# Rows of f2 scores by transposing a broadcast column, and routed rows of the first sixteen batches gathered inside the expert stage

## What is computed

```python
# experts: top 2 of softmax(x @ Wr), weights renormed; y = shared(x) + sum_e w_e * expert_e(x)
def _gat(inp, adj_mask, W, a):
    h = inp @ W;  f1 = h @ a[:F_, 0];  f2 = h @ a[F_:, 0]
    e = leaky_relu(f1[:, :, None] + f2[:, None, :], 0.2)      # masked in the second one
    return elu(softmax(e, axis=2) @ h)
out = relu(x @ mlp1_w + mlp1_b)                               # 256 wide
out = elu(_gat(relu(out), None, W_fc, a_fc)) + out
out = relu(out @ mlp2_w + mlp2_b)                             # 128 wide
out = elu(_gat(relu(out), adj, W_hand, a_hand)) + out;  return relu(out)
```

## Time and profile before

| what | us |
|---|---|
| median of 3 runs (1116.24 to 1118.69) | 1116.54 |
| the profiled execution | 1119.85 |
| its span, first to last instruction | 1118.1 |
| PE busy | 975.7 |
| DVE busy | 737.7 |
| ACT busy | 675.1 |
| POOL busy | 481.2 |

### The profile page before, as it was taken

The page is one execution under the profiler, slowest core; times in us unless marked ns, Lnnn a source line. Parts: engine busy times, 40 slices in busy tenths (PEclk is TensorE's granted clock), DMA queues, the critical chain, the costliest instruction groups (busy, mean ns, idle before and its releaser), DMA issues. The chain is left out here.

```text
span 1118.1 us, 25162 instructions
## 1 busy us (share of the span) xinstructions
PE 975.7 (87%) x7980; PEld 817.2 (73%) x7980; DVE 737.7 (66%) x2234; ACT 675.1 (60%) x1670; POOL 481.2 (43%) x474
## 2 busy tenths in 40 slices
PE   1698999997999999999999925899999998459998
PEld 1577888886667799999999922666666665349997
DVE  4678888885650145555545523588898896569998
ACT  4445666654433446666656613688888887467773
POOL 2545666651154654444400057677766722011111
PEclk9879999999999999999999966999999999779999
DMA  7900100112613137766565411111111100001011
GB/s 201 373 6 32 47 38 38 38 40 77 175 58 121 53 115 206 206 207 201 175 180 176 127 47 47 30 36 30 32 34 29 32 5 1 1 1 39 29 38 47
DMA packets 91705, 94.14 MB, mean 84 GB/s; under 512 B 16336, under 2 KB 69712, under 8 KB 90448
## 3 DMA queue, kind: packets, MB, share of 16 engines
q1 hardware_dynamic: 71936, 50.40, 14.4%
q10 hardware_dynamic: 11472, 25.63, 7.9%
q0 software_dynamic: 8192, 16.79, 4.9%
HBM read 52.54 MB, written 33.96 MB: 77 GB/s over the span
## 5 line engine op out<-in xcount | busy, mean ns | idle before, releaser
L1548 POOL DMA_INDIRECT g_y<-slot_rows_out,slots x128 | 129.6, 1012 | 141.3 <-SPq L1977 92.1
L1283 POOL DMA_INDIRECT slot_rows_in<-xn_all,slots x128 | 129.7, 1013 | 136.8 <-DMA slot_rows_in<-xn_all,slots 93.6
L1170 ACT ACTIVATE s_hT<-s_hp,expert 128x256 f32<-128x256 f32 x284 | 111.8, 476 | 54.6 <-PE s_hp L1161 54.5
L1183 PE MATMUL s_yp<-w_experts,s_hT 128*128 x1136 | 138.0, 275 | 0.0
L1183 PEld LDWEIGHTS s_yp<-w_experts,s_hT 128*128 128x128 f32 x1136 | 132.8, 192 | 0.0
L1191 DVE TENSOR_TENSOR xnT_all<-s_yp,expert 128x256 f32<-128x256 f32 x71 | 30.1, 424 | 117.7 <-PE s_yp L1183 117.7
L489 DVE SCALAR_TENSOR_TENSOR l_mi<-l_sbc,mT 128x512 bf16<-128x512 f32 x128 | 84.5, 670 | 7.1 <-PE l_sbc L480 5.9
L1159 PE MATMUL s_hp<-e_xh,e_wh 128*128 128x256 f32 x284 | 86.6, 305 | 0.0
L1082 ACT ACTIVATE s_hT<-s_hp,b_shared 128x512 f32<-128x512 f32 x64 | 44.0, 687 | 65.3 <-PE s_hp L1065 63.7
L1160 PE MATMUL s_hp<-e_xl,e_wh 128*128 128x256 f32 x284 | 80.5, 284 | 0.0
L1161 PE MATMUL s_hp<-e_xh,e_wl 128*128 128x256 f32 x284 | 80.5, 284 | 0.0
(11 more groups left out here) (323 smaller groups left out, 2652.7 us busy)
## 6 DMA issues: line engine op xcount, KB each, us to landing
expert<-expert_rows ACTq DMA_DIRECT2D x65, 322.0 KB, 3.1
slot_rows_in<-zeros SPq DMA_DIRECT2D x9, 1024.0 KB, 12.8
xnT_all<-slot_rows_in SPq DMA_DIRECT2D x71, 128.0 KB, 3.1
slot_rows_out<-xnT_all SPq DMA_DIRECT2D x71, 128.0 KB, 2.3
xn_all<-l_xr SPq DMA_DIRECT2D x16, 256.0 KB, 2.3
xnT_all<-l_rT SPq DMA_DIRECT2D x16, 256.0 KB
out_dram<-f_ot SPq DMA_DIRECT2D x16, 256.0 KB, 2.3
w_experts<-in_L_ffn_W2p_dram SPq DMA_DIRECT2D x8, 256.0 KB, 3.8
```

What stands on the lines that cost most here:

```text
L1170: nc.scalar.activation(hT[q % 2][:, c, :], hp[:, c, 0:TILE], ACT.Gelu, bias=wt[q][:, F + c:F + c + 1]).then_inc(s["h_ok"], 1)
L1183: ins = pe.matmul(yp[q % 2][:, h * D:(h + 1) * D], hT[q % 2][:, c, h * P:(h + 1) * P], w2, start=(c == 0 and h == 0), stop=(c == FC - 1), ...
L1283: pool.indirect_dma_start(k.rows_in, bass.IndirectOffsetOnAxis(ap=k.slots[:, c, b:b + 1], axis=0), k.xn[:, b, :], None).then_inc(scattered ...
L1548: pool.indirect_dma_start(y_slot[c][:, b, :], None, k.rows_out, bass.IndirectOffsetOnAxis(ap=k.slots[:, c, b:b + 1], axis=0))\
```

## The change

Four parts.

1. Both f2 rows are made from the h products: a second extra column is f2 as a column, and a PE transpose of this column, broadcast over 128 columns, gives it as a row on all partitions. Four transposes of 128 columns take the place of the products of 512 columns (two with a 256-deep weight for b, one for d). They read h1 and h2 in SBUF, and so wait for their evictions. w_f2_fc and w_f2_hand go, with the two copies that filled them.
2. PE's order: the f2 of d moves behind b_sums, the f2 of b behind the transposes of p2 and the dense layer of a.
3. Rows of batches 0 to 15 are gathered in the expert stage, by POOL, behind the scatter, once the last tile that holds such rows is stored (a place worked out from the slot counts by DVE, PE and DVE; y_ok is the gate). All gathered rows now lie in xn_all and xnT_all. The graph stage gathers groups 4 to 15 only, group 4 at its start, group g + 6 in step g.
4. slot_rows_out is zeroed in the attention stage by nine 1 MB DMAs on SP's queue, one behind the saves of each of the first nine groups.

```diff
                 for g in range(GROUPS):
                     sp_keep(sp, g)
+                    if g < k.zero_dmas:
+                        some = rows[:, 2048 * g:min(2048 * g + 2048, rows.shape[1])]
+                        sp.dma_start(some, k.zeros[:, 0:some.shape[1]]).then_inc(k.out_zeroed, 16)
...
+GATHERED_EARLY = 2
+def slot_rows(k, c, b):
+    return k.xn[:, b, :] if c == 0 else k.xnT[:, (b + 2 * AHEAD * TILE // P) % BATCHES, :]
...
         def pe_table(pe):
             pe.wait_ge(s["marks"], 1)
+            pe.transpose(counts[0:EC, 16:16 + J], last_of[:], k.ident[0:J, 0:J])
...
+                pool.wait_ge(s["table"], 1)
+                for n in range(TOPK * CHUNK * EC):
+                    b, c = n // TOPK, n % TOPK
+                    if n % (TOPK * CHUNK) == 0:
+                        at = b // CHUNK
+                        stored = pool.value_load(last_at[at:at + 1, 0:1], min_val=1 + U, max_val=TILES + U)
+                        pool.wait_ge(s["y_ok"], stored)
+                        pool.tensor_tensor(gather_fence[:, at:at + 1], k.ones[:, 0:1], k.ones[:, 0:1], ALU.mult)
+                    wait(pool, early[c], 16 * b)
+                    if n % IN_A_ROW == 0:
+                        wait(pool, early[1 - c], 16 * b)
+                    pool.indirect_dma_start(
+                        slot_rows(k, c, b), None, k.rows_out,
+                        bass.IndirectOffsetOnAxis(ap=k.slots[:, c, b:b + 1], axis=0)).then_inc(early[c], 16)
...
+                fold(dve.tensor_scalar(after_place[:], place[:], float(1 + U), None, ALU.add))
+                fold(dve.scalar_tensor_tensor(holds[:], counts[here, 128:128 + EC * EXPERTS]
+                                              .rearrange("p (c e) -> p c e", e=EXPERTS), j_start[here],
+                                              after_place[:].unsqueeze(1).to_broadcast([J, EC, EXPERTS]),
+                                              ALU.is_gt, ALU.mult))
+                dve.tensor_reduce(last_of[:], holds[:], AX.X, ALU.max)
...
+                fold(dve.tensor_reduce(last_f[:], counts[0:EC, 16:16 + J], AX.X, ALU.max))
+                dve.tensor_copy(last_at[:], last_f[:])
...
                 tiles(dve_slot, dve)
+                for q in range(U):
+                    dve.wait_ge(out[q], 16 * len(range(q, TILES, U)))
+                dve.memset(store_fence[:], 0.0).then_inc(s["y_ok"], U)
...
-W1C = FD + 1
+W1C = FD + 2
-W2C = D + 1
+W2C = D + 2
...
         def pe_b_f2(pe, g, p):
             wait(pe, s["y1_ok"], g)
             wait(pe, s["y2_ok"], g - 1)
-            for c in range(H1):
-                ins = pe.matmul(ff[:], k.w_f2_fc[:, c, :], r1T[p][:, c, :], start=(c == 0), stop=(c == H1 - 1))
+            for b in range(GB):
+                wait(pe, s["h1_ok"], g * GB + b + 1)
+                ins = pe.transpose(ff[:, b * P:(b + 1) * P], h1[p][:, b, FD + 1:FD + 2].to_broadcast([P, P]), k.ident[:])
             ins.then_inc(s["f1_ps"], 1)
...
-            pe.matmul(ff[:], k.w_f2_hand[:], r2T[p][:], start=True, stop=True).then_inc(s["f2_ps"], 1)
+            wait(pe, s["h2_ok"], g + 1)
+            for b in range(GB):
+                ins = pe.transpose(ff[:, b * P:(b + 1) * P], h2[:, b, D + 1:D + 2].to_broadcast([P, P]), k.ident[:])
+            ins.then_inc(s["f2_ps"], 1)
...
             if on["d"]:
                 pe_d_h2(pe, g, p)
-                pe_d_f2(pe, g, p)
             if on["c"]:
                 pe_b_sums(pe, g + 1, q)
+            if on["d"]:
+                pe_d_f2(pe, g, p)
             if on["b"]:
                 pe_b_h1(pe, g + 2, p)
             if on["a"]:
                 pe_a_transpose(pe, g + 3)
-            if on["b"]:
-                pe_b_f2(pe, g + 2, p)
             if on["d"]:
                 pe_d_transpose(pe, g)
             if on["a"]:
                 pe_a_dense(pe, g + 3)
+            if on["b"]:
+                pe_b_f2(pe, g + 2, p)
...
-                pool_gather(pool, 0, range(8))
-                for g in range(-4, GROUPS):
+                pool_gather(pool, FIRST, range(8))
+                for g in range(-2, GROUPS):
                     on = stages(g)
-                    more = g + 5 < GROUPS
+                    more = -1 <= g < GROUPS - FIRST - 2
                     if more:
-                        pool_gather(pool, g + 5, range(0, 6))
+                        pool_gather(pool, g + FIRST + 2, range(0, 6))
```

More of the change, by code:

```diff
@@ L812, in _ @@
                 sp.wait_ge(k.slots_zeroed, 16 * k.zero_dmas)
+                rows = k.rows_out.rearrange("(p n) d -> p (n d)", p=P)
                 for g in range(GROUPS):
                     sp_keep(sp, g)
+                    if g < k.zero_dmas:
+                        some = rows[:, 2048 * g:min(2048 * g + 2048, rows.shape[1])]
+                        sp.dma_start(some, k.zeros[:, 0:some.shape[1]]).then_inc(k.out_zeroed, 16)
+                sp.wait_ge(k.out_zeroed, 16 * k.zero_dmas)
                 sp.wait_ge(s["xr_kept"], 16 * GROUPS)
@@ L881, in persistent @@
     k.slots_zeroed = ctx.enter_context(nc.semaphore("slots_zeroed"))
+    k.out_zeroed = ctx.enter_context(nc.semaphore("out_zeroed"))
     k.zero_dmas = 9
@@ L993, in experts_phase @@
         pool_fence = sb("r_pool_fence", [P, CHUNKS])
+        EC = GATHERED_EARLY
+        j_start, after_place = sb("r_j_start", [P, 1]), sb("r_after_place", [J, EXPERTS])
+        holds, last_of = sb("r_holds", [J, EC, EXPERTS]), sb("r_last_of", [J, EC])
+        last_f, last_at = sb("r_last_f", [EC, 1]), sb("r_last_at", [EC, 1], I32)
+        store_fence, gather_fence = sb("r_store_fence", [P, 1]), sb("r_gather_fence", [P, EC])
         s_hT = [sb(f"s_hT{p}", [P, FC, GB * P]) for p in range(2)]
@@ L1020, in experts_phase @@
         scattered = [sem(f"m_scattered{p}") for p in range(2)]
+        early = [sem(f"m_early{c}") for c in range(TOPK)]
         x_in = [sem(f"m_x_in{q}") for q in range(U)]
@@ L1288, in _ @@
                 pool.memset(pool_fence[:, CHUNKS - 1:CHUNKS], 0.0).then_inc(s["arrived"], 1)
+                pool.wait_ge(s["table"], 1)
[12 more added lines that the diff above has]
+                        bass.IndirectOffsetOnAxis(ap=k.slots[:, c, b:b + 1], axis=0)).then_inc(early[c], 16)
+                for c in range(TOPK):
+                    pool.wait_ge(early[c], 16 * CHUNK * EC)
             @block.scalar
@@ L1493, in combine_graph_phase @@
         G4 = [P, GB, P]
-        y_slot = [sb(f"y{c}", [P, BATCHES, D]) for c in range(TOPK)]
+        FIRST = GATHERED_EARLY * CHUNK // GB
         st, fence, lnv = sb("st", [P, GB, 6]), sb("fence", [P, 1]), sb("lnv", [P, GB])
@@ L1540, in pool_gather @@
         def pool_gather(pool, g, which):
+            later = g - FIRST
             for n in which:
@@ L1544, in pool_gather @@
                 if n < TOPK:
-                    wait(pool, gathered[1 - g % 2][c], 16 * GB * ((g + 1) // 2))
+                    wait(pool, gathered[1 - g % 2][c], 16 * GB * ((later + 1) // 2))
                 else:
-                    wait(pool, gathered[g % 2][c], 16 * (GB * (g // 2) + n // TOPK))
-                pool.indirect_dma_start(y_slot[c][:, b, :], None, k.rows_out,
+                    wait(pool, gathered[g % 2][c], 16 * (GB * (later // 2) + n // TOPK))
+                pool.indirect_dma_start(slot_rows(k, c, b), None, k.rows_out,
                                         bass.IndirectOffsetOnAxis(ap=k.slots[:, c, b:b + 1], axis=0))\
@@ L1552, in dve_n_combine @@
         def dve_n_combine(dve, g, half, p, c):
-            wait(dve, gathered[p][c], (half + 1) * 16 * GB)
+            wait(dve, gathered[p][c], (half + 1 - FIRST // 2) * 16 * GB)
             if c == 1:
@@ L2006, in _ @@
                     if more:
-                        pool_gather(pool, g + 5, range(6, 8))
+                        pool_gather(pool, g + FIRST + 2, range(6, 8))
                     if on["b"]:
@@ L2283, in build @@
                 experts_phase(nc, k, a)
-        combine_graph_phase(nc, k)
+            combine_graph_phase(nc, k)
         last_ffn_phase(nc, k, out)
```

13 lines of the change are left out of this document (5 added, 8 removed).

## The result

The changed kernel takes 1190.96 us (median of 4 runs, 1190.74 to 1193.69), the kernel before 1116.39 beside it (4 runs, 1106.9 to 1118.69): 1.0691 times as long, 95% interval 1.0627 to 1.0754. Forecast were 1182 and a range of 1152 to 1206. The profiled execution took 1190.86 us, its span is 1189.1, 71.0 more than before. The page first: busy time by engine, then tenths in 40 slices of some 30 us.

A forecast was written before the change was run, and what follows sets the result against it. It took the ring of handovers through ACT, not PE throughput, as the bound. Loop 58.6, ramp -14.8 and clock 22 gave +65.8 us, 1185.7 for the profiled execution, 1182 as median; range 1152 to 1206.

The forecast's parts named there:

- The ring: Graph loop: handovers among ACT, DVE, POOL and PE bound the 16.77 us step; later operands for ACT lengthen it fully.
- d side: Graph loop: f2 of d behind b_sums lets ACT begin y2 1.2 us late each step.
- b side: Graph loop: f2 of b behind p2 transposes and dense layer lets ACT begin y1 3.1 us late each step.
- Step 13: Graph loop step without a dense layer on either side: 4.2 - 1.7 = 2.5 us longer.
- step 14: Graph loop step with only the d delay: 1.2 us longer.
- The ramp: Graph stage start to first h2: earlier gathers save 9.0 and 8.2 us, late f2 costs 1.2 twice: -14.8 us.
- The clock: Graph loop: new PE gaps lower the granted clock, a little over one fall a step, 1.6 x 14 = 22 us.
- Rival (b): Graph loop: the clock falls at both gaps in each step, 41 us for 22, total 1201; chance 0.15.
- Rival (a): Graph loop: the granted clock holds, +43.8 us, total 1160; chance 0.27.
- Costed at nothing: Early gathers behind the scatter, their gate's work and the nine zero DMAs: taken as 0 us.
- rival (d): Expert stage: early rows come too late as the gate opens with the last tile, +17.2, total 1199; chance 0.04.
- rival (e): Attention stage: zero DMAs delay the saves by some us each, +10 to 20, total 1197; chance 0.03.

The follow-up runs named there:

- e10: Changed kernel with unread products filling PE's three gaps and gathers of groups 5 to 15 left out: 1161.73 us, 1.038 times the kernel before.
- e8: Changed kernel with PE's old order, f2 of d as a product, f2 of b as transposes: 1096.28 us, 0.9815 times the kernel before.
- e11: Changed kernel with f2 of d back behind h2 and products filling the gaps before p2's and r2T's transposes: 1144.87 us, 1.0263 times the kernel before.
- e5: Changed kernel with two unread products of 512 columns in each of PE's three gaps: 1174.11 us, 1.0441 times the kernel before.
- e9: Changed kernel with fourteen transposes of ident in each of PE's three gaps: 1170.67 us, 1.0392 times the kernel before.
- e1: Changed kernel with both f2 rows as products in PE's old order, early gathers and zeroing kept: 1094.8 us, 0.9799 times the kernel before.
- e6: Changed kernel with f2 of b back between the transposes of xn and p2: 1136.73 us, 1.0115 times the kernel before.
- e3: Changed kernel with its f2 transposes kept but PE's order as before: 1104.02 us, 0.9886 times the kernel before.
- e7: Changed kernel with f2 of d back right behind h2, f2 of b still late: 1192.73 us, 1.0608 times the kernel before.

## Why the prediction was right, step by step

**The ring, and PE at 93% not the bound.** Shown: a step at full clock is 21.03 (forecast 16.77 + 4.2 = 21.0), e10 gives it with PE 93% busy, e8 gives 16.73 with PE 86% busy. The reading behind it, that ACT's small waits are the latency of a ring and no slack, held.

**d side 1.2, b side 3.1.** ACT's waits are 1.29 and 3.05 us, and by the step lengths (e11's table) it is 1.29 and 3.07. The prediction's 1.2 for the d side is kind and place in one: of the 1.29 the place behind b_sums is 0.93, and 0.36 is what the transposes cost over the product even right behind h2. The 0.46 us for four transposes of a broadcast column, which had no row, is 719.23 - 718.79 = 0.44. Step 13, forecast at 16.77 + 2.5 = 19.3, takes 18.6 in e5, e9 and e10; step 14, at 18.0, takes 17.9 (its clock is low in the kernel before too, 0.80, and 0.71 here). The fifteen without the new falls of the clock, 13 x 21.03 + 18.6 + 17.9, make 309.9 us, 58.3 over 251.57; of the 58.6 forecast 58.3 belong to these fifteen. e10 measures the same stretch with 311.7 us.

**The ramp.** -15.5 for -14.8, but as two misses that nearly cancel: without late f2 rows (e1) it is 43.1 - 62.44 = -19.3 where I had -17.2, and the f2 rows add 46.89 - 43.1 = 3.8 where I had 2.4.

**The clock: the term that was mis-sized.** 22 us were forecast, 343.63 - 309.9 = 33.7 came. The price of a fall, up to 1.45 us, was near (1.50 and 1.55, and 0.31 more behind them); their number was not. I took 1.6 us a step, a little over one fall; ten of the thirteen full steps are 2.7 us or more above 21.03, one is 0.75 above, and only two have none. Rival (b), a fall at both gaps of each step at 41 us, names the mechanism better than my count does, and the time lies about midway between its 1201 and my 1182. I had given weight against it to the stretch 952:957, where PE was idle and the clock stayed: one gap at the loop's end told little of gaps that return each step. Rival (a), the clock at 1.00 and 1160 us, did not happen; e10, at 1161.73, is about that kernel, its gathers aside. The gaps before the p2 and the r2T transposes are the ones with slow work behind them, as the prediction had it; the one before the third h1 product, 1.78 us, has none in any step of the changed kernel (it has in e6, where it grows to 3.5 us).

**Costed at nothing.** The gathers behind the scatter ended 23.6 us before POOL's next work, though each took 2.1 us for 1.4: rival (d) is out. The attention phase ended 1.37 us earlier than before (278.49 for 279.86, SP's mark), and SP waited 124.6 us for xr where it waited 127.5: rival (e) finds no cost. That the zeroing is free by itself was not run alone. The tile stage ended 4 us earlier than in the profile of before, where PE waited 2.88 us for a tile at the scatter's end; runs of the kernel before differ by as much (1106.9 to 1118.7), so I count it as no effect; no run settles it.

The sum by measured terms: 58.3 + 33.7 - 15.5 - 5.7 + 0.1 = 70.9 us, and by the spans it is 71.0. That the total came within 9 us of the forecast is in part luck: the clock was forecast 11.7 us too low, and the 5.7 us ahead of the graph stage, for which the prediction had nothing, took half of that back.

## What to carry to other kernels

Before operations of a busy engine are made cheaper or moved, follow what each result releases: in a loop where two engines hand work back and forth several times a step, an operand's place in the queue counts at its whole delay, and PE's busy share of 93% did not show what bounds it. A move that opens repeated gaps on TensorE is priced with a range, from no fall of the clock to a fall behind each gap, with the price of one from a row of such work at the low level; filling the gaps with work that is at hand tests it. Where a change has two halves, time each alone: here one half gave -2%, the other +9%.

## What the runs showed of the hardware

- Gaps of 1.78, 2.31 and 2.14 us in a step of 21 bring the granted clock down in eleven of thirteen steps (changed kernel). Gaps of at most 0.69 us did not in the twelve steps of e10, nor did one of 1.87 us a step (e8), nor 0.83 and 1.87 us (e3). In e6 the clock fell behind five gaps of 3.47 to 3.55 us, and not in the seven steps where that gap was 1.78 to 2.95. In e7 it was 0.81, the lowest, with gaps of 0.83, 2.31 and 2.13. So the length of a gap does not settle by itself whether it costs anything, and I can't predict which does.
- Fourteen 128x128 transposes in a gap held the clock nearly as well as two products of 512 columns did (e9 0.99, with one fall in twelve steps; e5 1.00).
- With indirect gathers in flight ACT began y2 up to 1.8 us later behind its finished operand (waits of up to 3.1 for 1.29 us; e5 against e10, and e6 before and behind its last gather), in steps at full clock; why is open.
- Under the tile loads 32 indirect gathers took 67 us, 2.1 each, for about 1.4 alone.
